# Windowed attention on one Trainium2 core: blocks of 14 rows by 8 columns in place of 2 rows by 56, with V relaid by column strips

## What is computed

```
B, H, W, C = x.shape                      # 4, 56, 56, 256
nh, K, lr = 8, 7, 4                       # heads, window, channels of q and k per head
q = (x @ Wq + bq).reshape(B, nh, H, W, lr) * scale
k = (x @ Wk + bk).reshape(B, nh, H, W, lr)
v = (x @ Wv + bv).reshape(B, nh, H, W, 32)
start_h = clip(arange(H) - 3, 0, H - K)   # the same for start_w
attn = einsum('bhijc,bhikjlc->bhijkl', q, k_win) + bias     # bias from rpb by relative place
attn = softmax(attn.reshape(B, nh, H, W, K * K), axis=-1)
out = einsum('bhijkl,bhikjld->bhijd', attn, v_win)
x = x + out.transpose(...).reshape(B, H, W, C) @ Wp + bp
```

## Time and profile before

| what | us |
|---|---|
| three runs, median | 9359.82 |
| lowest, highest | 9354.99, 9363.51 |
| the profiled execution, its own time | 9364.43 |
| its span in the profile | 9362.5 |
| project: start of the span to the attention's barrier | about 0 to 376 |
| attend: barrier to the next stage's first DMA | about 376 to 2500 |
| everything behind | 2500 to 9362.5 |

### The profile page before, as it was taken

The page is one execution under the profiler, slowest core; times in us unless marked ns, Lnnn a source line. Parts: engine busy times, 40 slices in busy tenths (PEclk is TensorE's granted clock), DMA queues, the critical chain, the costliest instruction groups (busy, mean ns, idle before and its releaser), DMA issues. The chain is left out here.

```text
span 9362.5 us, 159380 instructions
## 1 busy us (share of the span) xinstructions
PE 8337.6 (89%) x48656; PEld 4762.7 (51%) x48656; DVE 5718.6 (61%) x13462; ACT 4384.1 (47%) x9478; POOL 3594.7 (38%) x2306
## 2 busy tenths in 40 slices
PE   4399998999898999999999999999999988448777
PEld 3255554555565545555454555545455334347666
DVE  3355555555467977677676777767677203446666
ACT  1055555555421045655565555656555663023333
POOL 3000000000011046666666666666666665443333
PEclk8655555555697589999999999999999999678889
DMA  5411112110285011211212111121201103311110
GB/s 150 87 14 22 22 22 39 22 22 8 77 254 171 0 29 30 52 34 37 49 33 52 34 44 39 34 52 33 62 23 33 37 4 114 115 46 43 47 43 25
DMA packets 439338, 480.69 MB, mean 51 GB/s; under 512 B 163096, under 2 KB 401290, under 8 KB 434151
## 3 DMA queue, kind: packets, MB, share of 16 engines
q1 hardware_dynamic: 415015, 426.26, 18.9%
q0 software_dynamic: 23424, 43.45, 1.6%
HBM read 298.78 MB, written 180.34 MB: 51 GB/s over the span
## 5 line engine op out<-in xcount | busy, mean ns | idle before, releaser
L1182 DVE TENSOR_REDUCE a_tops<-a_ps 128x1 f32<-128x448 f32 (+1 forms) x5600 | 3071.4, 613 | 1085.7 <-PE a_ps L1084 1068.4
L1282 ACT ACTIVATE a_P<-a_ps 128x448 f32<-128x448 f32 (+1 forms) x5600 | 2656.1, 547 | 2116.1 <-PE a_ps L1153 2083.7
L1305 POOL TENSOR_TENSOR a_added<-a_P 128x896 f32<-128x896 f32 x1344 | 2799.9, 2102 | 2087.3 <-ACT a_P L1282 2087.3
L1153 PE MATMUL a_ps<-a_qp,a_kp 98*128 98x448 f32 (+1 forms) x5600 | 2155.1, 400 | 98.5 <-ACT a_P L1282 73.2
L1084 PE MATMUL a_ps<-a_hk,a_hq 96*128 96x448 f32 (+1 forms) x4900 | 1818.4, 381 | 0.8 <-DMA a_hq<-scratch_q 0.7
L1153 PEld LDWEIGHTS a_ps<-a_qp,a_kp 98*128 98x128 f32 (+1 forms) x5600 | 1029.9, 187 | 1290.3 <-ACT a_P L1282 737.4
L1104 PE MATMUL a_ps<-a_P,a_vt 128*32 128x448 f32 (+1 forms) x11200 | 1334.5, 548 | 0.0
L461 DVE CUSTOM_DVE_ANT_0 n_sm<-n_ps,n_bias 112x448 f32<-112x448 f32 x928 | 578.2, 624 | 851.4 <-PE n_ps L392 851.4
L1084 PEld LDWEIGHTS a_ps<-a_hk,a_hq 96*128 96x128 f32 (+1 forms) x4900 | 916.2, 187 | 262.1 <-DVE a_tops L1182 170.7
L487 ACT ACTIVATE n_P<-n_sm,n_mx 112x448 f32<-112x448 f32 x928 | 619.9, 668 | 843.5 <-DVE n_mx L461 843.5
L402 PE MATMUL n_ps<-n_idn,n_P 112*112 112x112 f32 x3712 | 923.9, 405 | 21.5 <-DVE n_P L468 21.5
(11 more groups left out here) (195 smaller groups left out, 8124.0 us busy)
## 6 DMA issues: line engine op xcount, KB each, us to landing
a_qp<-scratch_q SPq DMA_DIRECT2D x168, 224.0 KB, 3.9
a_kp<-scratch_k SPq DMA_DIRECT2D x96, 320.0 KB, 5.1
a_hk<-scratch_k SPq DMA_DIRECT2D x84, 336.0 KB, 5.0
scratch_t<-o_ts SPq DMA_DIRECT2D x56, 448.0 KB, 5.1
a_hq<-scratch_q SPq DMA_DIRECT2D x84, 200.0 KB, 3.2
e_w<-in_w SPq DMA_DIRECT2D x16, 1024.0 KB, 6.8
a_hq<-scratch_q SPq DMA_DIRECT2D x84, 192.0 KB, 3.4
p_xs<-in_x SPq DMA_DIRECT2D x4, 3136.0 KB, 15.3
```

Source lines behind the costliest of these rows:

```text
L1153: pe.matmul(PS[0:rows_of(t), i_s % 3, 0:GW], kp[0:98, hh, 128 * t:128 * t + rows_of(t)], qp[0:98, hh, GW * j:GW * j + GW], start=True, sto ...
L1182: dve.tensor_reduce(tops[0:rows_of(t), KT * hh + t, k:k + 1], PS[0:rows_of(t), bank, 0:GW], AX_X, ALU.max).then_inc(topped, 1)
L1282: act.activation(P[0:rows_of(t), (2 * n + pair) % (2 * RING), hh % 2, :], PS[0:rows_of(t), (4 * n + hh) % 3, 0:GW], ACT.Exp).then_inc(expe ...
L1305: pool.tensor_tensor(added2[:, a % 6, :, :], P[:, (2 * n + pair) % (2 * RING), :, :], P[:, (2 * n + 2 + pair) % (2 * RING), :, :], ALU.add ...
```

## The change

In the attention the queries of a head go in blocks of 14 rows by 8 columns: 4 row blocks by 7 column blocks make 28 blocks (`NBLK`) of 112 queries, and the keys of a block are 20 rows by 14 columns, 280 in all. The step is now a block with all its four heads: four score matmuls, one in each row strip and each into its own PSUM bank (0 to 3), then twelve transposes of 98 columns of P (three chunks that begin at 0, 98 and 182, so that the third overlaps the second by 14 keys, for which V has zeros), then twelve V matmuls into one bank (`OUT` = 7). Transposes use banks 4 to 6 in turn. The numbers of steps: 896 in place of 928.

V is stored in DRAM by head group and token (`v0`), and 14 DMAs for each image copy it within DRAM into `vw`, in which each column block's 14 columns lie together. The attention loads V from there straight into the layout of the matmul, three DMAs for each row block, in two buffers. The projection makes V in 32 groups of 98 tokens in place of 28 of 112 and stores it in two halves. GpSimd places q and k, in four pieces an iteration, while the iteration before still runs; the bias is written in the final layout (126 DMAs in place of 64) and loaded without a copy.

The diff's core (line numbers of the kernel after are those of the order below):

```diff
@@ layer0_project, SP @@
-                sp.wait_ge(v_read, (b + 1) * NT)
-                sp.dma_start(S["v0"][b].rearrange("(j p) c -> p j c", p=TT), vs[:, :, :]).then_inc(stored, 16)
-                sp.wait_ge(stored, (b + 1) * 48)
+                for g in range(2):
+                    sp.wait_ge(v_read, b * VT + 16 * (g + 1))
+                    sp.sem_inc(steps, 1)
+                    sp.dma_start(S["v0"][b, g].rearrange("(m t s) d -> t m (s d)", m=4, s=SUB), vs[:, 4 * g:4 * g + 4, :])\
+                      .then_inc(stored, 16)
+                sp.wait_ge(stored, (b + 1) * 64)
                 sp.sem_inc(image_done, 1)
+                for g in range(2):
+                    for tc in range(COL_BLOCKS):
+                        sp.dma_start(S["vw"][b, g, tc].rearrange("(r c) d -> r c d", c=14),
+                                     S["v0"][b, g].rearrange("(r c) d -> r c d", c=W)[:, KEY_COL[tc]:KEY_COL[tc] + 14, :])\
+                          .then_inc(relaid, 16)
+            sp.wait_ge(relaid, B * 2 * COL_BLOCKS * 16)
@@ layer0_attend, SP @@
+            def load_values(g, b, rb):
+                for m in range(3):
+                    skip = 14 if m == 2 else 0
+                    at = slice(14 * KEY_ROW[rb] + CHUNK_FROM[m] + skip, 14 * KEY_ROW[rb] + CHUNK_FROM[m] + CHUNK)
+                    sp.dma_start(vt[skip:CHUNK, rb % 2, :, m, :], S["vw"][b, g][:, at, :].rearrange("x p d -> p x d"))\
+                      .then_inc(v_loaded[rb % 2], 16)
...
+            sp.wait_ge(zeroed, 3)
+            load_qk(0, 0)
+            load_bias(0, 0)
+            load_values(0, 0, 0)
             sp.dma_start(idn[:, :], A["eye"][0:TT, 0:TT]).then_inc(consts, 16)
@@ layer0_attend, TensorE @@
+            def scores(it, n):
+                rb, tc = divmod(n, COL_BLOCKS)
+                if tc == 0 and rb < 3:
+                    pe.wait_ge(placed, it * 8 + 4 + 2 * rb)
+                since(pe, maxed, it, U, 4 * n)
+                for hh in range(4):
+                    rows = slice(32 * hh, 32 * hh + 16)
+                    pe.matmul(PS[0:TT, hh, 0:KEYS].rearrange("p (r c) -> p r c", c=14), qp[rows, n, :],
+                              kp[rows, KEY_ROW[rb]:KEY_ROW[rb] + 20, KEY_COL[tc]:KEY_COL[tc] + 14],
+                              start=True, stop=True).then_inc(scored, 1)
+            def turn(it, n):
+                for hh in range(4):
+                    m = 4 * n + hh
+                    pe.wait_ge(normed, it * U + m + 1)
+                    since(pe, copied, it, U, bank_free_at(m) + 1)
+                    for c, k0 in enumerate(CHUNK_FROM):
+                        last = pe.transpose(PS[0:CHUNK, turn_bank(m), TT * c:TT * c + TT], P[:, m % 8, k0:k0 + CHUNK],
+                                            idn[:, :])
+                    last.then_inc(turned, 1)
+            def mix(it, n):
...
+                since(pe, out_read, it, NBLK, n)
+                for c in range(3):
+                    for hh in range(4):
+                        last = pe.matmul(PS[32 * hh:32 * hh + 32, OUT, 0:TT], vt[:, rb % 2, tc, c, 32 * hh:32 * hh + 32],
+                                         PTs[:, (4 * n + hh) % 8, TT * c:TT * c + TT], start=(c == 0), stop=(c == 2))
+                last.then_inc(mixed, 1)
+            def body(it, first):
+                for n in range(NBLK):
+                    scores(it, n)
+                    if n >= 1:
+                        turn(it, n - 1)
...
+                    if n >= 2:
+                        mix(it, n - 2)
@@ layer0_attend, VectorE @@
+            def normalise(it, n, pair):
+                m = 4 * n + 2 * pair
+                dve.wait_ge(exped, it * U + m + 2)
+                dve.reciprocal(rc[:, m % 8:m % 8 + 2], rs[:, m % 8:m % 8 + 2]).then_inc(inverted, 1)
+                dve.wait_ge(inverted, it * (U // 2) + m // 2 + 1)
+                for k in (m, m + 1):
+                    dve.tensor_scalar(P[:, k % 8, :], P[:, k % 8, :], rc[:, k % 8:k % 8 + 1], None, ALU.mult)\
+                       .then_inc(normed, 1)
+            def body(it, first, fresh):
+                for n in range(NBLK):
...
+                    maxima(it, n)
+                    normalise(it, n, 0)
+                    if n >= 2:
+                        read_out(it, n - 2)
...
+                    normalise(it, n, 1)
@@ layer0_attend, ScalarE @@
+            def body(it):
+                for n in range(NBLK):
+                    exponentials(it, n)
+                    copy_turned(it, n)
```

More of the change, by code:

```diff
@@ L162, in _ @@
-            pool.wait_ge(tables_written, 16 * (NH + W + n))
+            pool.dma_start(S["toeplitz"].rearrange("c s r w -> (c s) (r w)"), far[0:3 * SUB, 0:NH * RPB * 14])\
+                .then_inc(tables_written, 16)
+            for h in range(NH):
+                pool.dma_start(S["bias"][h].rearrange("o p f -> p o f"),
+                               far[0:TT, :].rearrange("p (o f) -> p o f", o=9)).then_inc(tables_written, 16)
+            pool.wait_ge(tables_written, 16 * (NH + 1))
+            pool.wait_ge(filled, 2)
@@ new lines, in load_bias, with store @@
+            def load_bias(g, rk):
+                for hh in range(4):
+                    sp.dma_start(bias[:, hh, 3 * rk:3 * rk + 3, :],
+                                 S["bias"][4 * g + hh, 3 * rk:3 * rk + 3].rearrange("o p f -> p o f"))\
+                      .then_inc(bias_loaded[rk], 16)
+            def store(g, b, it, rb):
+                sp.wait_ge(out_read, it * NBLK + 7 * (rb + 1))
+                sp.sem_inc(steps, 1)
+                since(sp, stored, it, 4 * 16, 16 * rb)
+                if not isinstance(it, int):
+                    sp.sem_inc(steps, 1)
+                at = slice(14 * W * rb, 14 * W * (rb + 1))
+                sp.dma_start(S["y0T"][b * 2 + g][:, at], yT[:, at]).then_inc(stored, 16)
@@ new lines, in body @@
+            def body(g, b, before, after, switch=False, switched=False):
+                it = g * B + b
+                for rb in range(ROW_BLOCKS):
+                    since(sp, mixed, it, NBLK, 7 * rb)
+                    if not isinstance(it, int):
+                        sp.sem_inc(steps, 1)
+                    if rb < ROW_BLOCKS - 1:
+                        load_values(g, b, rb + 1)
+                    elif after is not None:
+                        load_values(after[0], after[1], 0)
+                    if rb > 0:
+                        store(g, b, it, rb - 1)
+                    elif before is not None:
+                        store(*before, it - 1, ROW_BLOCKS - 1)
+                    if rb == 0 and after is not None:
+                        sp.wait_ge(placed, it * 8 + 8)
+                        if not isinstance(it, int):
+                            sp.sem_inc(steps, 1)
+                        load_qk(*after)
+                    if switch and rb == 1:
+                        load_bias(1, 0)
+                    if switch and rb == 3:
+                        load_bias(1, 1)
+                    if switched and rb == 0:
+                        load_bias(1, 2)
@@ new lines, in maxima @@
+            def maxima(it, n):
+                rb, tc = divmod(n, COL_BLOCKS)
+                case = 3 * ROW_CASE[rb] + COL_CASE[tc]
+                for hh in range(4):
+                    m = 4 * n + hh
+                    since(dve, exped, it, U, m - 3)
+                    dve.wait_ge(scored, it * U + m + 1)
+                    dve.sem_inc(steps, 1)
+                    dve.tensor_tensor_reduce(out=sm[:, hh, :], in0=PS[0:TT, hh, 0:KEYS], in1=bias[:, hh, case, :],
+                                             scale=1.0, scalar=3.0e38, op0=ALU.add, op1=ALU.min,
+                                             accum_out=mx[:, m % 8:m % 8 + 1]).then_inc(maxed, 1)
@@ new lines, in body @@
+            def body(it, first, fresh):
+                for n in range(NBLK):
+                    if fresh and n in (0, 7, 21):
+                        dve.wait_ge(bias_loaded[(0, 7, 21).index(n)], (it // B + 1) * 64)
+                    maxima(it, n)
+                    normalise(it, n, 0)
+                    if n >= 2:
+                        read_out(it, n - 2)
+                    elif not first:
+                        read_out(it - 1, NBLK - 2 + n)
+                    normalise(it, n, 1)
@@ L498, in _, with exponentials @@
-        @block.gpsimd
-        def _(pool):
-            with pool.Fori(0, 2 * B) as it:
-                pool.wait_ge(loaded, (it + 1) * NLOAD)
-                pool.sem_inc(steps, 1)
-                pool.tensor_copy(kp[:, :, :], kn[:, :, :]).then_inc(keys_placed, 1)
-                pool.wait_ge(scored, (it + 1) * U)
+            def exponentials(it, n):
+                for hh in range(4):
+                    m = 4 * n + hh
+                    act.wait_ge(maxed, it * U + m + 1)
+                    since(act, turned, it, U, m - 7)
```

(4 more changed lines are left out.)

361 lines of the change are left out of this document (150 added, 211 removed).

## The result

The kernel after takes 8468.55 us (median of four runs, 8467.22 to 8475.56), against 9361.67 for the kernel before beside it: a ratio of 0.9048, with a 95% interval of 0.9032 to 0.9063. The forecast was 8525 with 8370 to 8740. The profiled execution has a span of 8473.8 us, 888.7 less than before.

A forecast was written before the change was run, and what follows sets the result against it. It took TensorE's work at the low clock of 1.2 GHz as the attention's bound. Attention compute -880, its start -43 and projection +88 make -835 from 9364.4, so 8529, predicted as 8525, range 8370 to 8740.

The forecast's parts named there:

- TensorE's block, 4.3: Attention: scores 0.50, transposes 2.53 and V 1.29 make 4.3 us of TensorE for four heads, against 8.4 before.
- The chain, 5.0 a block: Attention: next exponentials wait for ScalarE's copies of this block, so a block takes 5.0 us; 224 blocks make 1120.
- Placing is hidden: Attention: GpSimd's placing of q and k costs nothing, since it has a row block of 35 us for each piece.
- The turns, 25 us: Attention: seven loop turns, with the refill of the chain, cost 3.5 us each, 25 in all.
- The stage's term, 1153 us in 224 blocks and the turns: Attention compute: 1153 us in place of 2033, so -880, with fill and tail of 8 included.
- The start, -43: Start of the attention: first load to first matmul takes about 35 us in place of 78.8, so -43.
- The projection, +88: Projection: V groups +14, the store's shorter tail -22, copies within DRAM exposed four times at 24 us, +96; sum +88.
- Rival 1: Attention scores: row strips do not overlap, scores cost 2.0 us a block, +200, about 8725; chance 20%.
- Rival 2: Attention: PSUM evacuation and softmax set the pace, through higher clock or overlap; 4.3 a block, -157, about 8370; chance 10%.
- Rival 3: Projection: the copies for V are hidden behind the next image, 72 us less, about 8455; chance 7%.
- The four semaphore steps: Attention scores: a semaphore step for each score matmul, 149 ns for four, up to 33 us in all.
- Rival 4: Attention: lock step, blocks and strips not overlapping, 8.9 us a block, 9400, slower than before; chance 2%.

The follow-up runs named there:

- e11: Kernel after with blocks of the old width: 448 keys, four transposes and four V chunks a head; 8703.19 us, measured once.
- e3: Kernel after with the scores of all four heads taken from the first row strip; 8501.25 us.
- e5: Kernel after with ScalarE reordered: two exponentials, last two copies of the block before, other two exponentials, first two copies; 8390.25 us.
- e1: Kernel after with the next image's load issued ahead of the 14 copies within DRAM; 8416.73 us.
- e4: Kernel after with TensorE's old order at the new sizes: for each head one score, its transposes, one V chunk; 9236.48 us.
- e8: Kernel after with the attention's eight iterations written out, no loop instruction on TensorE, VectorE and ScalarE; 8426.37 us.
- e10: Kernel after with image load first, ScalarE's other order, identity's load first, no attention loops, placing left on GpSimd; 8289.22 us.

## Why the prediction was right

The sign, the size (-893 measured by the medians, -835 forecast) and the order of the terms were right. Point by point:

- **What bounds it.** TensorE at 1.2 GHz, with a change of kind three times a head. Right in the main: with the new order alone the block falls to 5.85. But of that fall the scores side by side are the larger part and the changes of kind behind transposes and V products the smaller (e11, e3). And 1.2 GHz held for most of the new stage only: the forecast took 0.50 throughout, and 0.59 was granted.
- **TensorE's block, 4.3.** Measured 4.27 by the lengths, and 4.19 in e5, with each of its three terms within 0.12.
- **The chain, 5.0 a block.** Right in its members, since moving ScalarE's copies took the waits away (e5), but 0.36 too long: I had the first transposes at 1.69 us behind the first exponential, where my own terms add up to 1.62 and 1.78 was measured (1007.61 - 1005.83; the multiply lasts 0.365 and not 0.29). Yet the last copy lets the next exponential start 4.64 behind the first, not 4.87, and the 0.13 on top for the read-out was not there. That is 81 us in 224 blocks, the largest error of the sum.
- **Placing is hidden.** This step failed. I named GpSimd's time as its cover and did not ask what VectorE does meanwhile. The long blocks cost 57 us, and the run without placing is 74 faster. The trace of the kernel before had the sign of it, seven times over: beside GpSimd's copy of the keys a multiply of 450 ns lasts 2.80 us.

```profile
695.94 2.80 POOL L503 CAST n_kp<-n_kn 128x3136 fp32r<-128x3136 f32 x1 [253.37 <-PE n_ps L392]
...
696.18 2.80 DVE L468 TENSOR_SCALAR n_P<-n_P,n_rc 112x448 f32<-112x448 f32 x1
```

- **The turns, 25 us.** Six of them cost 6.4 each, not seven 3.5.
- **The stage's term, 1153 us in 224 blocks and the turns.** It came to 1111.6, and four errors stood in it. From the times of the blocks in TensorE's timeline, an estimate of each:

| part of the stage | forecast | measured |
|---|---|---|
| 224 blocks at their steady pace | 1120 | 1039 |
| GpSimd's placing | 0 | 57 |
| turns | 25 | 38 |
| blocks at 2.4 GHz | 0 | -28 |
| filling, tail and the rest | 8 | 5 |

That the sum fell within 41 us of the forecast is in part luck: two of the errors are of one sign and two of the other. At 1.2 GHz throughout it would have been within 15.

- **The start, -43:** -38, and it waited for the identity, as said.
- **The projection, +88:** +71. The load did wait behind the copies (e1). The term that was too large is the copies': SP's issue of 15 us and the longer landing make about 20 an image, where I took 24. The load lands in 22.7 us and not near 40, the sign that I had named, because most of the delay stands ahead of its issue: the copies take SP 15.7 us, and the two together are 38. The 37.0 us from which I had the slow bound for the copies are what GpSimd spent on issuing its DMAs, not the time of their transfers; the sum does not use them.
- **Rival 1** does not occur, and I had its price far too high: one strip costs 0.69 us of TensorE, not 1.5, and 33 us in all, not 200. The range reached to 8740 on its account.
- **Rival 2** (a block of 4.3) is where e5 leads, through an edit that the change does not hold. The higher clock that it names came too, for 42 blocks, without an edit.
- **Rival 3** does not occur but is there to be had: e1 is this rival, -52 for my -72.
- **The four semaphore steps**, which the sum left out, did not show ahead of the first minimum: it begins 0.75 us behind the start of the four scores, and 0.76 behind that of a single score in e4.
- **Rival 4**: the mechanism exists. In e4 the longer work of TensorE and a wait in each block bring it to 8.2 us, close to the 8.7 from which the change would lose. It is the order in TensorE's queue that keeps it away, as I argued.

## What to carry to other kernels

Where an in-order engine alternates kinds of work, count the changes of kind and ask first whether a bigger step can group them, and whether what is grouped can then run side by side; both together were worth twice the smaller window here. Then look at which engine's order holds the next step's first instruction behind this step's last one, and let half of the next go ahead. And where an idle engine takes over copies, ask whom it slows, not only whether it has time: the longest duration of an instruction beside its median can show it in the trace of before.

## What the runs showed of the hardware that I had not expected

- GpSimd's copies in SBUF stretch VectorE's multiply from SBUF to SBUF from at most 370 ns to as much as 2301, and leave its minima, which read PSUM, alone. The multiply ends 161 to 168 ns behind a copy's end, so it waits for the whole copy. The Trainium skill, GPSIMD Engine Reference, in its table of specifications, has GpSimd's SBUF interfaces shared with VectorE, with contention where VectorE's instruction is in a 2-port mode or has two SBUF inputs; the rows agree that the multiply and the copies collide; which of the two cases the multiply is, no run here shows.
- Four matmuls in one row strip have all but the first of their weight loads hidden: 1.19 us for four with 280 columns at 1.2 GHz, against 0.50 in four strips.
- A jump back in the attention's loops costs the kernel 6.4 to 7 us (e8), where the engines show 2.4 to 4.7 of issue each.
- The granted clock rises for a few blocks at a time in a stage that had 0.50 throughout before (0.57 over 1000 to 1500 us, 0.66 over 700 to 1000 in e10). Why it rises was not tried.
